# GpSimd waits for each chunk's gathered rows to land before it issues the next chunk's gathers, in both edge layers of a graph network

## What is computed

```python
h = jnp.maximum(_layernorm(x, axis=-1), 0.0)
# layer 0: a row of a table per (node, relation), one per edge, summed by destination
h_all = jnp.einsum('nd,rdf->nrf', h, weight)                    # 8 relations
gate_all = jnp.einsum('nd,rdo->nro', h, gate_weight)[..., 0]
msg = h_all[src, rel_type] * norm * jax.nn.sigmoid(gate_all[src, rel_type])[:, None]
x = x + jax.nn.relu(jax.ops.segment_sum(msg, dst, num_segments=6250))

h = jnp.maximum(_layernorm(x, axis=-1), 0.0)
# layer 1: an MLP on each edge's 64 features, a time gate, and the gathered node row
ef = (jax.nn.relu(edge_attr @ We1 + be1) @ We2 + be2) * jax.nn.sigmoid(ts @ Wt + bt)
combined = jnp.concatenate([h[row], ef], axis=1)
msg = jax.nn.relu(combined @ Wn1 + bn1) @ Wn2 + bn2
x = x + jax.ops.segment_sum(msg, col, num_segments=6250) + h
```

## Time and profile before

| | us |
|---|---|
| median of 3 runs | 8255.84 |
| lowest and highest of them | 8231.78, 8259.04 |
| profiled execution, first to last instruction | 8249.1 |
| layer 0's edge stage, first gather to last closed chunk | 318.2 to 2962.5 |
| layer 1's edge stage, first gather to last `z` | 3061.4 to 6210.7 |

### The profile page before, as it was taken

One profiled execution on the slowest core, in us unless ns is written; L12 is line 12 of the kernel. 1 busy time (PEld: TensorE's weight loads), 2 busy tenths in 40 slices (PEclk: granted clock), 3 DMA queues, 4 the chain that ended last, 5 costly groups with the idle time before them and its releaser, 6 DMA issues. The chain is left out here.

```text
span 8249.1 us, 107364 instructions
## 1 busy us (share of the span) xinstructions
PE 6558.1 (80%) x25772; PEld 3855.2 (47%) x25773; DVE 3342.9 (41%) x11422; ACT 2319.1 (28%) x5705; POOL 3151.3 (38%) x3263
## 2 busy tenths in 40 slices
PE   0766666666666639999999999999996996999999
PEld 0333333333333325555565556555554443444444
DVE  6566666666666643333333333333333113000000
ACT  0244444444444422222222222222221012111100
POOL 0266555655556534445444454444450000000000
PEclk9765555555556555555555555555565998999999
DMA  1322222222222223333333332333331542655565
GB/s 47 144 72 72 71 72 71 72 71 72 71 72 72 71 64 87 83 85 86 83 83 83 83 88 81 84 84 84 85 87 46 165 158 91 195 172 193 172 195 165
DMA packets 464073, 811.21 MB, mean 98 GB/s; under 512 B 222120, under 2 KB 236418, under 8 KB 460823
## 3 DMA queue, kind: packets, MB, share of 16 engines
q1 hardware_dynamic: 288300, 407.74, 15.7%
q0 software_dynamic: 103968, 213.28, 10.1%
q10 hardware_dynamic: 71728, 189.18, 7.2%
HBM read 697.41 MB, written 110.80 MB: 98 GB/s over the span
## 5 line engine op out<-in xcount | busy, mean ns | idle before, releaser
L1015 POOL DMA_INDIRECT e_rows<-scratch_table,e_staged x1616 | 1544.3, 956 | 1694.7 <-DVE e_z L1153 903.0
L615 POOL DMA_INDIRECT e_rows<-scratch_table,e_staged x1616 | 1585.7, 981 | 1353.3 <-DVEq L227 596.8
L551 PE MATMUL e_banks<-hi_hot,lo_hot 128*128 128x392 bf16 x3138 | 1074.0, 494 | 705.3 <-remote 330.5
L519 DVE TENSOR_SCALAR hi_hot<-iota_hi,key 128x392 bf16<-128x392 f16 x3138 | 1071.1, 341 | 13.1 <-issue 12.6
L160 PEld LDWEIGHTS e_win<-e_onehot,e_msg 128*128 128x128 f32 x3232 | 729.2, 313 | 503.4 <-issue 347.6
L551 PEld LDWEIGHTS e_banks<-hi_hot,lo_hot 128*128 128x128 bf16 x3138 | 355.1, 132 | 1230.1 <-issue 515.2
L160 PE MATMUL e_win<-e_onehot,e_rows 128*128 128x64 f32 x3232 | 680.0, 384 | 279.1 <-issue 226.3
L1095 ACT ACTIVATE e_msg<-e_z 128x512 f32<-128x512 f32 x404 | 254.4, 630 | 2251.3 <-DVE e_z L1153 2073.6
L160 PEld LDWEIGHTS e_win<-e_onehot,e_rows 128*128 128x128 f32 x3232 | 691.7, 304 | 410.1 <-issue 369.9
L518 DVE TENSOR_SCALAR lo_hot<-iota_lo,key 128x128 bf16<-128x128 bf16 x3138 | 779.0, 248 | 202.5 <-remote 138.6
L1040 PE MATMUL e_p<-e_edge,we 64*128 64x512 f32 x808 | 756.8, 1034 | 129.9 <-issue 106.2
(11 more groups left out here) (189 smaller groups left out, 6203.7 us busy)
## 6 DMA issues: line engine op xcount, KB each, us to landing
ring<-scratch_counts SPq DMA_DIRECT2D x336, 896.0 KB, 4.7
e_time<-in_time_rows ACTq DMA_DIRECT2D x404, 256.0 KB
e_rows<-scratch_table,e_staged POOLq DMA_INDIRECT x3232
e_edge<-in_edge_T SPq DMA_DIRECT2D x404, 128.0 KB
scratch_counts<-h ACTq DMA_DIRECT2D x12, 3136.0 KB
scratch_counts<-type_mem ACTq DMA_DIRECT2D x12, 3136.0 KB
scratch_table<-table_tile SPq DMA_DIRECT2D x49, 512.0 KB, 2.6
e_staged<-idx SPq DMA_DIRECT2D x404, 2.0 KB
```

Source lines behind the costliest of these rows:

```text
L519: return nc.vector.tensor_scalar(hi_hot, iota_hi[:, :], key[:, 1:2], None, ALU.is_equal)
L551: return nc.tensor.matmul(bank, lo_hot[:, slot, :], hi_hot[:, slot, :], start=start, stop=stop)
L615: pool.indirect_dma_start(rows[:, b, j, :], None, A["table0"], bass.IndirectOffsetOnAxis(ap=staged[:, b, j:j + 1], axis=0),).then_inc(rows ...
L1015: pool.indirect_dma_start(rows[:, b, j, :], None, A["table1"], bass.IndirectOffsetOnAxis(ap=staged[:, b, j:j + 1], axis=0),).then_inc(rows ...
```

## The change

One instruction is added to each of the two functions that issue a chunk's gathers: after the fourth gather POOL waits until `rows_in[b]` has the value that it has when all four have landed.

```diff
@@ layer 0
                                     rows[:, b, j, :], None, A["table0"],
                                     bass.IndirectOffsetOnAxis(ap=staged[:, b, j:j + 1], axis=0),
                                 ).then_inc(rows_in[b], 16)
+                            pool.wait_ge(rows_in[b], base + 16 * J * o + 16 * J)
```

## The result

| | us |
|---|---|
| changed kernel, median of 4 runs | 8573.36 (8567.73 to 8578.81) |
| kernel before, median of 4 runs beside it | 8247.6 (8231.78 to 8259.04) |
| ratio, with 95% interval | 1.0394 (1.0373 to 1.0416) |
| forecast, with its range | 8735 (8580 to 8880) |

The change costs 326 us, 3.9%. The sign and the mechanism in layer 0 are as forecast; the forecast was 162 us too high and its range missed the result by 7 us.

A forecast was written before the change was run, and what follows sets the result against it. The consumer bounds both edge layers before; POOL's 7.37 us cycle would bound layer 0 after. 8249.1 + 335 (layer 0) + 144 (stores) + nothing (layer 1) = 8728 us profiled, forecast 8735 us, range 8580 to 8880.

The forecast's parts named there:

- The sign: Whole kernel: slower than before by more than 25 us, chance 0.95.
- the mechanism in layer 0: Layer 0: POOL's chain of issue, landing and wake, 7.37 us per chunk, exceeds the consumer's 6.54, so POOL becomes the bound.
- What bounds the kernel: Edge layers before: the consumer sets the pace, 6.54 us per chunk in layer 0 and 7.78 in layer 1, not POOL.
- POOL's cycle: Layer 0 after the change: issue 4.82, pauses 0.13, landing 1.55, wake 0.87, together 7.37 us per chunk, bounds 7.04 to 7.85.
- Landing and wake: POOL's chain behind a chunk's last gather: landing 1.55 us plus wake 0.87 us, together 2.42 us.
- The Trainium skill's fit: Gathers: about 2.0 us plus bytes / 436e3, 2.15 us for 64 KB; cycle 6.99 us, total some 150 us less.
- The stores: Layer 0's 24 stores of counts delay gather landings in POOL's chain: 6 us each, +144 us, bounds 50 and 185.
- Layer 1 "at nothing": Layer 1: POOL's cycle of 7.29 us stays 0.49 under the consumer's 7.78, so the wait costs nothing.
- 970 us of new waits: Layer 1: 404 x (1.6 + 0.8) us of landing and wake lie inside time POOL would wait for `z` anyway.
- The rival "faster": Layer 0: spacing gathers removes DVE's 405 us of remote stalls if POOL's cycle is under 6.54; 8119 us, chance 0.01.
- Sum: Whole kernel: 8249.1 + 335 + 144 = 8728 us for the profiled execution, forecast 8735 us, 6.7 us above it.

The follow-up runs named there:

- l0_only: The new landing wait in layer 0 alone, against the kernel before: 8634 us, ratio 1.0582.
- group 3: One chip: kernel before, changed kernel, and layer 1 fills of 1800 and 200 numbers, against the kernel before: ratios 1.0010, 1.0462, 0.9858, 0.9907.
- group 1: Landing wait in layer 0 alone, layer 1 alone, or for the previous chunk; or layer 1 fill; against kernel before: 1.0582, 0.9929, 1.0009, 0.9876.
- group 4: Kernel before unchanged, and with layer 1 fills: doubled after every second chunk, 900 numbers, 1800 numbers; ratios to before 0.9981, 1.0024, 0.9755, 0.9851.
- pause_both_s: Kernel before plus a POOL pause behind each chunk's gathers, fills of 900 numbers in layer 1 and 200 in layer 0: 7878 us, ratio 0.9574.
- before_c: The kernel before, unchanged, run again for its profile on another chip: 8175 us, ratio 0.9981.

## Why the prediction was wrong

- **What bounds the kernel.** Right: in `l0_only` and the changed kernel POOL becomes the bound of layer 0, and PE waits for rows in nearly every chunk (383 of 404).
- **POOL's cycle.** Right: 7.37 us forecast, 7.39 measured without the stores. Landing and wake were 2.47 us where the sum had 2.42. The Trainium skill's fit in "DMA: Bandwidth & Descriptors" ("Anatomy of one DMA — SWDGE (gpsimd) path"), by which the cycle would be 6.99, is too short for these gathers: the trace does not agree, and the measured cycle decides.
- **The stores** were mis-sized: 144 us forecast, 60 measured. The forecast weighed two cases, a gather that lands up to 7.7 us late and one that keeps its place ahead of the store and costs about 2, and took 6 us for every store. The rows show both cases: POOL's one long wait per store is over the ordinary 2.5 us by about 1 us for 12 of the 24 stores of the changed kernel and by 3.5 to 5.8 us for the other 12. Where in a cycle the store falls decides it. In the changed kernel and in `l0_only` every store issued up to 4.1 us behind its chunk's first gather (16 of them) has a long wait behind it, and every one from 4.34 us on, with the fourth gather well under way, a short one; in between there are both.
- **Layer 1 "at nothing"** is the step that failed: it gained 107 us in the first pair of profiles (58 in group 3 and 95 in group 1). I priced the wait as a loss hidden by idle time, 7.29 us against 7.78, which is right as a mean: but a chunk of this stage takes 7.9 or 4.3 us by PE's clock in the rows of group 4, and over the second kind POOL does run back to back. Holding it back there goes with fewer stalls of DVE (164 us with a remote cause before, 93 after) and with more work done at full clock. That pausing POOL brings the gain is shown; that it comes through the stalls is only in part. The recorded sentence also sets the 970 us of new waits inside 903 us of idle time, which is less; what carries that step is the comparison of the two cycles alone.
- **The rival "faster"** named this mechanism, from the earlier trace rows, for layer 0 only, and tied it to a cycle under 6.54. In layer 0 of the changed kernel the remote idle time before that add is gone altogether (405 us before), but POOL's cycle hides what that is worth. Where both conditions held was layer 1, which the rival left out. `pause_both_s`, whose layer 0 runs at 2503 / 403 = 6.21 us per chunk, has a POOL cycle under the 6.54 us and shows the rival's condition and its gain.
- **Sum.** From first to last closed chunk the forecast for layer 0 is 403 x 7.37 + 144 = 3114 us, and 3062 were measured: 52 too high. These are 84 too much for the stores, less 9 for the cycle without them, less 24 by which the changed kernel's layer 0 is longer than that of `l0_only`. Most of the 24 are the stores again, as `l0_only` has 7 long waits where the changed kernel has 12, and the excess of the 24 waits over 2.46 us is 52 us against 72. Layer 1 adds 107, and the rest of the program takes off 8: 151 us between the forecast span of 8728 and the measured 8577. The forecast of 8735 is 162 too high, since the profiled execution lies 7 us under the median before and 3 us over it after.

## What to carry to other kernels

A wait for a transfer in the queue that issues the next one costs landing and wake per turn (here 2.5 us), and only as far as the whole chain, here 7.4 us, is over the consumer's pace; waiting for the transfer before that one cost nothing that could be measured here. Compare that chain with the consumer's pace in each of its regimes, not only with the mean. And look at what a queue that runs ahead does to the others: a short pause behind each four gathers (a fill of 0.3 or 0.9 us, and the wait for it) was worth 4.3% on one chip, where the landing wait cost 3.9 and 4.6% in its two pairs of runs, so a producer that catches up in bursts can be worth slowing down to a cycle just under the consumer's. Look for the stalls first: on the chip that showed none the short pause in layer 1 gained nothing, and longer ones in layer 1 and in both layers cost 5.0 and 8.3%.

## What the hardware showed that I had not expected

- The same program took 7417 us on one chip and 8171 to 8248 us in the five other sets of runs, with a granted clock over layer 0 of 0.75 against 0.59 in the two that are shown. The chip with the higher clock has no DVE wait with a remote cause in either edge stage, even where POOL issues gathers without a break.
- In the two stretches of layer 1 that are shown, full clock ended beside idle time of PE: 4.73 us in the one, 3.4 of 10.2 us in the other. In the second it had come after 40.9 us in which PE was busy throughout.
- In `before_c`, DVE sat idle 137 us in 26 stalls, the longest 6.6 us, before one add of layer 1. In the stall that is shown, in the kernel before, the add's inputs had been there for some 6 us. A fill of 900 or 1800 numbers and the wait for it behind each four gathers takes these to 12 to 14 us; a fill of 200 leaves them standing and still gains.
